# A two-layer graph kernel: each normalised tile transposed and projected one aggregation later

## The chip, the cores and the metric

The kernel runs on one core of one Trainium2 chip. The metric is the device time in microseconds. A core has five engines that run side by side and meet through semaphores: TensorE (PE, matrix products and transposes), VectorE (DVE), ScalarE (ACT), GpSimd (POOL) and SyncE (SP, which here only issues DMAs).

## The reference

The input is `x` (16 graphs, 1024 nodes, 256 features) and `adj` (16 x 1024 x 1024 integers, here 0 or 1, symmetric, with ones on the diagonal). Layer 0 is a gated aggregation, layer 1 an attention-like one; each is added to its input and normalised over the features:

```python
# layer 0: e = leaky((h * a0) @ h.T), alpha = sigmoid(e) where adj == 1 (0 elsewhere)
x = _layernorm(x + (einsum('bij,bjd->bid', alpha, h) + bias))
# layer 1
Hh = einsum('bni,io->bno', h, W); s = Hh @ a_src; d = Hh @ a_dst
e = where(adj != 0, exp(-leaky_relu(s[:, :, None] + d[:, None, :])), 0)
x = _layernorm(x + elu(einsum('bnm,bmo->bno', e, Hh) / rowsum(e)))
```

## The kernel before, in words

A graph's 1024 nodes are eight tiles of 128. The 16 graphs are passes of one loop (graph 0 and the last one are written out, 1 to 14 are the hardware loop); every engine has its own list of instructions for a pass, written out by hand in its own function `graph(b, prev, nxt)`, and the engines meet only at semaphore waits. An engine works its list strictly in this written order. `prev` and `nxt` say whether there is a graph before and behind: parts of the neighbours' work are laid between.

A pass has two halves. **Layer 0** has one step per tile t:
- PE aggregates tile t (`aggregate0`, L1154): 8 source tiles times 3 products of split numbers (`split_products`, L1097 to L1101), 24 matmuls into one of two accumulation banks (`acc_bank`). It needs the coefficients (`lo0`) and, from t = 2, that DVE has taken the residual of tile t - 2 out of its bank (`resid0`).
- DVE takes the residual (`residual0`, L822), the statistics (L827) and moments (L832); POOL computes 1/sqrt(var + eps) (`power0`, L357, L360); DVE normalises the tile into `x1` (`norm0`, L839).
- PE transposes the normalised tile (`transpose_x1`, two transposes, L1172) into `xt_bank`; ACT copies it out rounded (`high_x1T`, L551, `x1T_hi`) and DVE computes what the rounding left (`low_x1T`, L844, `x1T_lo`).
- PE projects it with W (`project`): one transpose that spreads a column of the tile before (`spread_s`, L1179), then six matmuls into `hh_bank` (L1099 to L1101). ACT takes the result out (`keep_H`, L565 to L574, four or five short steps), which frees `hh_bank` for the next projection.
- In between stand the coefficients for tile t + 3 (PE's `mirror`, L1150; DVE's `mask0_below` and `mask0_rest`, L798, L807; ACT's `high0`, L541; POOL's `low0`, L349), the transposes and splits of the next graph's x (`transpose_x`, L1107; `high_xT`, L472, L475; `low_xT`, L745, L748), chunks of its scores (`scores_chunk`; ACT's `scale_scores`, L498; DVE's `leaky_scores`, L757), and the first halves of the layer 1 coefficients (`mask1_pair`, L873).

**Layer 1** aggregates again, eight times 8 matmuls (`aggregate1`, L1213), from `H` and the coefficients, and normalises and stores.

In the kernel before, PE handles tile 0 of `x1` behind aggregation 2 and tiles 1 to 5 around aggregations 3 to 7: at step t it transposes tile t - 2 ahead of aggregation t and projects it behind it. Tiles 6 and 7 come behind the loop, with score chunks 2 to 5 of the next graph laid between. DVE's `low_x1T` and ACT's `high_x1T` and `keep_H` stand at the steps that match. `xt_bank` and `hh_bank` are single; `x1T_hi` and `x1T_lo` have two slots.

POOL's and SP's lists are not touched. SP's queue stores finished tiles and loads the next x; POOL's issues the loads of `adj`.

Of the kernel before, what the change touches and what calls it, by code (L numbers as in the profile page):

```python
# [116 lines left out]
def two_graph_layers(nc, x, adj, a0, a1, a2, a3, bias, W, a, out):  # L117
    B, N, D = x.shape
    NT = N // P
# [33 lines left out]
    with ctx:  # L153
# [309 lines left out]
        def _(act):  # L463
# [82 lines left out]
            def high_x1T(S, b, t, prev):  # L546
                act.wait_ge(S.x1T, NT * b + t + 1)

                if t >= 2 or prev:
                    act.wait_ge(S.proj, NT * b + t - 1)  # L550
                nc.scalar.activation(x1T_hi[:, t % 2, :, :],  # L551
                                     xt_bank[:, 0:D].rearrange("p (c i) -> p c i", c=KD),
                                     ACT.Copy).then_inc(S.x1T_hi, 1)
# [47 lines left out]
            def graph(b, prev, nxt):  # L601

                for t in range(NT + 1):
                    if t >= 3:
                        keep_H(F, b, t - 3, prev, False)
                    if t >= 2:
                        high_x1T(F, b, t - 2, prev)
                    if nxt and t in XT_STEP:
                        high_xT(F, b + 1, XT_STEP[t], False)
                    if t < 6:  # L610
                        watch_codes(b, t)
                    if 1 <= t and t + 3 < NT:
                        high0(F, b, t + 3, prev)
                    if t == 1 and prev:
                        norm1(F, b - 1, NT - 1)
                    if nxt and 6 <= t:
                        scale_scores(b + 1, t - 6)
                    if t in (6, 7):
                        watch_codes(b, t)

                keep_H(F, b, 6, prev, False)
                high_x1T(F, b, 7, prev)
                if nxt:
                    scale_scores(b + 1, 3)
                if nxt:
                    scale_scores(b + 1, 4)
                keep_H(F, b, 7, prev, False)
                ends_H(F, b)
                if nxt:
                    scale_scores(b + 1, 5)  # L630
                if nxt:
                    scale_scores(b + 1, 6)
                    keep_codes(F, b + 1, 0, True)
                last_G(F, b, False)
                if nxt:
                    scale_scores(b + 1, 7)
                    keep_codes(F, b + 1, 1, True)
                    high_x(F, b + 1, 0)
                    high_x(F, b + 1, 1)
                    keep_codes(F, b + 1, 2, True)  # L640

                for t in range(NT + 1):
                    if t >= 1:
                        elu_parts(F, b, t - 1)
                    if nxt and t == 0:
                        scale_scores(b + 1, 8)
                    if nxt and 1 <= t < 3:
                        tanh_row(b + 1, t - 1)
                        scale_row(b + 1, 2 + t)
                    if t + 3 >= NT and nxt:  # L650
                        high0(F, b + 1, t + 3 - NT, True)
                    if nxt:
                        if t + 3 < ACT_CODES:
                            keep_codes(F, b + 1, t + 3, True)
                        if t == 0:
                            high_x(F, b + 1, 2)
                            high_x(F, b + 1, 3)
                        if 3 <= t:
                            tanh_row(b + 1, t - 1)
                    if t >= 2:  # L660
                        norm1(F, b, t - 2)
# [55 lines left out]
        def _(dve):  # L717
# [204 lines left out]
            def graph(b, prev, nxt):  # L922

                for t in range(NT + 1):
                    if t >= 1:
                        residual0(F, b, t - 1, prev)

                    if 1 <= t < 3:
                        mask0_below(b, t + 3, prev)
                    if t >= 1:  # L930
                        stats0(F, b, t - 1)
                    if 2 <= t < 6:
                        low_x1T(F, b, t - 2)
                    if t >= 1:
                        moments0(F, b, t - 1)
                    if t >= 6:
                        low_x1T(F, b, t - 2)
                    if 3 <= t and t + 3 < NT:
                        mask0_below(b, t + 3, prev)
                    if 1 <= t and t + 3 < NT:  # L940
                        mask0_rest(b, t + 3)
                    if t == 6:
                        mask1_pair(b, 0, prev, 0, EDGE)
                    if t == 7:
                        mask1_pair(b, 2, prev, 0, EDGE)
                    if nxt and t == 5:
                        low_xT(F, b + 1, XT_STEP[t], False)
                    if t >= 1:
                        norm0(F, b, t - 1, prev)
                    if nxt and t < 5 and t in XT_STEP:  # L950
                        low_xT(F, b + 1, XT_STEP[t], False)
                    if nxt and 6 <= t:
                        leaky_scores(b + 1, t - 6)

                low_x1T(F, b, 7)
                if nxt:
                    leaky_scores(b + 1, 3)
                if nxt:
                    leaky_scores(b + 1, 4)
                mask1_pair(b, 0, prev, EDGE, NT)  # L960
                watch_sd(F, b, prev)
                if nxt:
                    leaky_scores(b + 1, 5)
                mask1_pair(b, 2, prev, EDGE, NT)
                if nxt:
                    leaky_scores(b + 1, 6)
                keep_watch(b, prev)

                for t in range(NT + 1):
                    if t >= 1:  # L970
                        row_inverse(F, b, t - 1, prev)
                    if t < 2:
                        mask1_pair(b, 2 * t + 4, prev)
                    if nxt and t == 1:
                        leaky_row(b + 1, 3)
                    if t + 3 >= NT and nxt:
                        mask0_below(b + 1, t + 3 - NT, True)
                        mask0_rest(b + 1, t + 3 - NT)
                    if nxt and ACT_CODES <= t + 3 < NT:
                        keep_codes(b + 1, t + 3)  # L980
                    if t >= 1:
                        residual1(F, b, t - 1)
                        stats1(F, b, t - 1)
                        moments1(F, b, t - 1)
                    if nxt and t in (0, 2):
                        leaky_row(b + 1, 2 + t)
# [109 lines left out]
        def _(pe):  # L1096
# [125 lines left out]
            def graph(b, prev, nxt):  # L1222

                for t in range(NT):
                    if t >= 3:

                        pe.wait_ge(F.x1T_lo, NT * b + t - 2)
                        transpose_x1(F, b, t - 2)
                    if 1 <= t and t + 3 < NT:
                        mirror(b, t + 3)  # L1230
                    aggregate0(F, b, t, prev)
                    if t == 2:
                        if prev:

                            pe.wait_ge(F.x1T_lo, NT * b)
                        transpose_x1(F, b, 0)
                    if t >= 3:
                        project(F, b, t - 2, prev)
                    if nxt and t + 1 in XT_STEP:
                        c = XT_STEP[t + 1]  # L1240
                        if c == 0:
                            pe.wait_ge(F.x_loaded, 16 * (b + 2))

                            pe.wait_ge(F.leaky, NCH * (b + 1))
                        if c >= 2:
                            pe.wait_ge(F.xT_lo, 4 * (b + 1) + c - 1)
                        transpose_x(F, b + 1, c)
                    if nxt and 5 <= t < 7:
                        if t == 5:
                            pe.wait_ge(F.xT_lo, 4 * (b + 1) + 3)  # L1250
                        else:
                            pe.wait_ge(F.xT_lo, 4 * (b + 1) + 4)
                        scores_chunk(b + 1, t - 5)
                    if t == 2:
                        project(F, b, 0, prev)

                pe.wait_ge(F.x1T_lo, NT * b + 6)
                transpose_x1(F, b, 6)
                if nxt:
                    scores_chunk(b + 1, 2)  # L1260
                    scores_chunk(b + 1, 3)
                project(F, b, 6, prev)
                pe.wait_ge(F.x1T_lo, NT * b + 7)
# [114 lines left out]
```

## Time and profile before

| | |
|---|---|
| median of 3 runs | 1476.43 us (1476.39 to 1477.39) |
| the profiled execution, its own time | 1477.27 us |
| its span, first to last instruction | 1474.8 us |
| PE busy | 1353.2 us, 92% |
| DVE busy | 1095.8 us, 74% |
| ACT busy | 934.7 us, 63% |
| POOL busy | 837.1 us, 57% |
| mean granted TensorE clock | 0.958 of full |

All 16 graphs share the span, so an average over it mixes the two halves of a pass. The share of an engine says how much it works, and not where it makes others late; for that one reads the waits, and then a single pass in order of time.

### The profile page before, as it was taken

What the parts mean: (1) busy time and instruction counts of PE and PEld (TensorE: products, weight loads), DVE (VectorE), ACT (ScalarE), POOL (GpSimd) and SP (SyncE); (2) the same over time, 40 slices, a digit from 0 to 9 for tenths busy, and PEclk for the clock granted to TensorE, in tenths of its full rate; (3) what the DMA queues carried; (4) which work ended last, traced back from release to release, by engine and by line L of the source; (5) the groups of instructions that cost most, each with busy time, mean ns of one, the idle gap of its engine ahead of it and who ended that gap; (6) DMA issues with size and microseconds to landing.
All of it is one profiled execution on the core that took longest, in us unless ns stands there. A gap on an engine that the chain in (4) does not pass through costs nothing.

```text
span 1474.8 us, 30279 instructions
## 1 busy us (share of the span) xinstructions
PE 1353.2 (92%) x9154; PEld 1231.1 (83%) x9154; DVE 1095.8 (74%) x2784; ACT 934.7 (63%) x2197; POOL 837.1 (57%) x1228
## 2 busy tenths in 40 slices
PE   4799998999989899898999989899898998989986
PEld 3688888988888798888988889798888988889875
DVE  4487876878777687776778777687777778778764
ACT  3676756657575665756757575666756756675642
POOL 3465737556484655737557383655737557384732
PEclk9799999999999999999999999999999999999988
DMA  4122130321303222131321303222121321303100
GB/s 103 30 44 64 31 67 28 50 61 32 71 15 50 65 43 64 23 53 48 50 61 32 72 15 50 65 39 64 26 50 51 50 61 26 74 19 50 36 1 31
DMA packets 55251, 68.73 MB, mean 47 GB/s; under 512 B 5488, under 2 KB 38640, under 8 KB 55152
## 3 DMA queue, kind: packets, MB, share of 16 engines
q0 software_dynamic: 18432, 33.56, 14.2%
q1 hardware_dynamic: 36720, 34.22, 7.2%
q14 instruction: 83, 0.68, 0.1%
q8 instruction: 16, 0.26, 0.1%
HBM read 84.55 MB, written 16.78 MB: 69 GB/s over the span
## 4 chain that ended last, share of the span: by engine, by line
PE 64%; DVE 13%; issue 8%; POOL 6%; DMA 5%; ACT 3%; DVEq 1%; SPq 0%; POOLq 0%; ACTq 0%
PE acc_bank L1213 23%; PE acc_bank L1099 6%; PE acc_bank L1100 6%; PE acc_bank L1101 6%; DMA code_nat<-in_adj 4%; PE lg_bank L1099 3%; PE lg_bank L1101 3%; PE lg_bank L1100 3%; DVE coef L873 3%; PE tr_bank L1134 3%; PE tr_bank L1150 3%; PE xt_bank L1172 2%; PE hh_bank L1101 2%; PE hh_bank L1099 2%; PE hh_bank L1100 2%
## 5 line engine op out<-in xcount | busy, mean ns | idle before, releaser
L1213 PE MATMUL acc_bank<-H,coef 128*128 128x258 f32 x2048 | 472.7, 384 | 9.0 <-ACT reluP L592 8.4
L1213 PEld LDWEIGHTS acc_bank<-H,coef 128*128 128x128 f32 x2048 | 383.4, 191 | 64.7 <-issue 10.9
L349 POOL TENSOR_TENSOR coef_lo<-coef,coef_hi 128x1024 fp32r<-128x1024 f32 x128 | 305.4, 2387 | 72.9 <-ACT coef_hi L541 71.7
L1099 PE MATMUL acc_bank<-h_hi,coef_hi 128*128 128x256 f32 x1024 | 309.3, 302 | 6.3 <-DVE resid L822 6.3
L1100 PE MATMUL acc_bank<-h_lo,coef_hi 128*128 128x256 f32 x1024 | 296.7, 290 | 0.0
L1101 PE MATMUL acc_bank<-h_hi,coef_lo 128*128 128x256 f32 x1024 | 295.8, 289 | 0.0
L873 DVE SCALAR_TENSOR_TENSOR coef<-G,E_col,codeT 128x256 f32<-128x256 f32 x512 | 238.0, 531 | 39.3 <-PE acc_bank L1213 36.6
L1099 PEld LDWEIGHTS acc_bank<-h_hi,coef_hi 128*128 128x128 f32 x1024 | 206.5, 202 | 9.3 <-issue 9.3
L1100 PEld LDWEIGHTS acc_bank<-h_lo,coef_hi 128*128 128x128 f32 x1024 | 206.6, 202 | 0.0
L1101 PEld LDWEIGHTS acc_bank<-h_hi,coef_lo 128*128 128x128 f32 x1024 | 205.4, 201 | 0.0
L541 ACT ACTIVATE coef_hi<-coef 128x1024 fp32r<-128x1024 f32 x128 | 136.3, 1065 | 99.0 <-DVE coef L807 98.8
L335 POOL DMA_DIRECT2D code_nat<-in_adj x128 | 73.6, 576 | 188.0 <-PE tr_bank L1134 167.3
L590 ACT ACTIVATE eluE<-acc_bank,rinv 128x256 f32<-128x256 f32 x128 | 60.8, 475 | 173.9 <-DVE rinv L897 173.9
L531 ACT ACTIVATE watch_junk<-codeT,neg_half 128x1024 bf16<-128x1024 bf16 x128 | 149.8, 1170 | 1.5
L366 POOL TENSOR_TENSOR neg_mean<-zero_col,moments 128x1 f32<-128x1 f32 x128 | 36.4, 284 | 198.7 <-DVE moments L920 198.7
L1099 PE MATMUL lg_bank<-hT_hi,gT_hi 128*128 128x384 f32 (+3 forms) x384 | 139.0, 362 | 3.9 <-DVE gT_lo L748 2.9
L498 ACT ACTIVATE score<-lg_bank 128x128 f32<-128x128 f32 (+2 forms) x192 | 95.1, 495 | 67.8 <-PE lg_bank L1101 67.7
L757 DVE TENSOR_TENSOR score<-lg_bank,score 128x128 f32<-128x128 f32 (+2 forms) x192 | 103.4, 551 | 41.5 <-ACT score L498 40.4
L1101 PE MATMUL lg_bank<-hT_hi,gT_lo 128*128 128x384 f32 (+3 forms) x384 | 132.2, 344 | 0.0
L1100 PE MATMUL lg_bank<-hT_lo,gT_hi 128*128 128x384 f32 (+3 forms) x384 | 131.6, 343 | 0.0
L357 POOL TENSOR_TENSOR var_eps<-moments,eps_col 128x1 f32<-128x1 f32 x128 | 43.0, 336 | 141.0 <-DVE moments L832 141.0
L1099 PE MATMUL hh_bank<-W_hi,x1T_hi 128*128 128x258 f32 x256 | 84.8, 331 | 27.1 <-DVE x1T_lo L844 27.1
(87 smaller groups left out, 2895.9 us busy)
## 6 DMA issues: line engine op xcount, KB each, us to landing
code_nat<-in_adj POOLq DMA_DIRECT2D x128, 256.0 KB, 3.6
x_raw<-in_x SPq DMA_DIRECT2D x16, 1024.0 KB, 5.5
out<-x SPq DMA_DIRECT2D x128, 128.0 KB, 1.7
score<-in_L_gnn_W SPq DMA_DIRECT2D x1, 256.0 KB, 2.8
score<-in_L_gnn_a SPq DMA_DIRECT2D x1, 256.0 KB, 5.8
bias_bc<-in_L_gnn_bias SPq DMA_DIRECT2D x1, 128.0 KB, 3.6
a_col<-in_L_gnn_a SPq DMA_DIRECT2D x4, 1.0 KB, 2.1
```

Of the source, the lines that this page charges most:

```text
L335: pool.dma_start(code_nat[:, t % 4, :], adj_v[b, t, :, :]).then_inc(S.adj_loaded[t % 4], 16)
L349: nc.gpsimd.tensor_tensor(coef_lo[:, t % 4, :, :], blocks(coef[:, t % 4, :]), f32(coef_hi[:, t % 4, :, :]), ALU.subtract).then_inc(S.lo0, 1)
L498: nc.scalar.activation(score_at(J, c0, c1), lg_bank[k % 2][:, 0:(c1 - c0) * P], ACT.Copy, scale=SLOPE).then_inc(F.scaled, 1)
L531: nc.scalar.activation(watch_junk[:, :], codeT[:, t, :], ACT.Square, bias=neg_half[:, :], accum_out=watch_sum[:, t:t + 1]).then_inc(F.code ...
L541: nc.scalar.activation(coef_hi[:, t % 4, :, :], blocks(coef[:, t % 4, :]), ACT.Copy).then_inc(S.hi0, 1)
L590: nc.scalar.activation(eluE[:, t % 2, :], acc_bank[t % 2][:, 0:D], ACT.Exp, scale=rinv[:, t % 2, :]).then_inc(S.elu_exp, 1)
L757: nc.vector.tensor_tensor(score_at(J, c0, c1), lg_bank[k % 2][:, 0:(c1 - c0) * P], score_at(J, c0, c1), ALU.max).then_inc(F.leaky, 1)
L873: ins = nc.vector.scalar_tensor_tensor(coef[:, at:at + 2, J * P:(J + 1) * P], blocks(G[:, t * P:(t + 2) * P]), E_col[:, J:J + 1], codeT[:, ...
L1099: nc.tensor.matmul(dst, lhs_hi, rhs_hi, start=first, stop=False)
L1100: nc.tensor.matmul(dst, lhs_hi, rhs_lo, start=False, stop=False)
L1101: return nc.tensor.matmul(dst, lhs_lo, rhs_hi, start=False, stop=last)
L1213: ins = nc.tensor.matmul(acc_bank[t % 2][:, 0:HC], coef[:, SLOT1[t], J * P:(J + 1) * P], H[:, J, :], start=J == 0, stop=J == NT - 1)
```

## The change

In layer 0 each tile of `x1` is transposed and projected one aggregation later: at step t PE transposes tile t - 3 ahead of aggregation t and projects it behind it. The special place of tile 0 behind aggregation 2 goes. Tiles 5, 6 and 7 come behind the loop, each with one score chunk between its transpose and its projection. `high_x1T`, `keep_H` (ACT), `low_x1T` and the first halves of `mask1_pair` (DVE) move by one step with it.

```diff
 # ACT, in graph()
                 for t in range(NT + 1):
+                    if t >= 4:
+                        keep_H(F, b, t - 4, prev, False)
                     if t >= 3:
-                        keep_H(F, b, t - 3, prev, False)
-                    if t >= 2:
-                        high_x1T(F, b, t - 2, prev)
+                        high_x1T(F, b, t - 3, prev)
...
+                keep_H(F, b, 5, prev, False)
+                high_x1T(F, b, 6, prev)
+                if nxt:
+                    scale_scores(b + 1, 3)
                 keep_H(F, b, 6, prev, False)
                 high_x1T(F, b, 7, prev)
-                if nxt:
-                    scale_scores(b + 1, 3)
                 if nxt:
                     scale_scores(b + 1, 4)
 # DVE, in graph()
-                    if 2 <= t < 6:
-                        low_x1T(F, b, t - 2)
+                    if 3 <= t < 6:
+                        low_x1T(F, b, t - 3)
                     if t >= 1:
                         moments0(F, b, t - 1)
                     if t >= 6:
-                        low_x1T(F, b, t - 2)
+                        low_x1T(F, b, t - 3)
...
-                    if t == 6:
+                    if t == 7:
                         mask1_pair(b, 0, prev, 0, EDGE)
-                    if t == 7:
+                    if t == 8:
                         mask1_pair(b, 2, prev, 0, EDGE)
...
+                low_x1T(F, b, 6)
+                if nxt:
+                    leaky_scores(b + 1, 3)
                 low_x1T(F, b, 7)
-                if nxt:
-                    leaky_scores(b + 1, 3)
 # PE, in graph()
                     if t >= 3:
-
-                        pe.wait_ge(F.x1T_lo, NT * b + t - 2)
-                        transpose_x1(F, b, t - 2)
+                        if t > 3 or prev:
+                            pe.wait_ge(F.x1T_lo, NT * b + t - 3)
+                        transpose_x1(F, b, t - 3)
                     if 1 <= t and t + 3 < NT:
                         mirror(b, t + 3)
                     aggregate0(F, b, t, prev)
-                    if t == 2:
-                        if prev:
-
-                            pe.wait_ge(F.x1T_lo, NT * b)
-                        transpose_x1(F, b, 0)
                     if t >= 3:
-                        project(F, b, t - 2, prev)
+                        project(F, b, t - 3, prev)
...
-                    if t == 2:
-                        project(F, b, 0, prev)
-
+
+                pe.wait_ge(F.x1T_lo, NT * b + 5)
+                transpose_x1(F, b, 5)
+                if nxt:
+                    scores_chunk(b + 1, 2)
+                project(F, b, 5, prev)
                 pe.wait_ge(F.x1T_lo, NT * b + 6)
                 transpose_x1(F, b, 6)
                 if nxt:
-                    scores_chunk(b + 1, 2)
                     scores_chunk(b + 1, 3)
                 project(F, b, 6, prev)
```

## Rows read from the trace of the kernel before

**Rows 1.** The page, part 1: busy time, share of the span, instructions

```profile
PE 1353.2 (92%) x9154; PEld 1231.1 (83%) x9154; DVE 1095.8 (74%) x2784; ACT 934.7 (63%) x2197; POOL 837.1 (57%) x1228
```

**Rows 2.** PE's waits in total: us, times, longest us

```profile
PE xt_bank L1172 <- DVE x L839: 27.3, 22, 1.7
PE hh_bank L1099 <- DVE x1T_lo L844: 27.1, 16, 1.9
```

**Rows 3.** PE in order of time, graph 7: start, us, what [idle before <- releaser]

```profile
687.62 0.41 PE L1172 MATMUL xt_bank<-ident,x 128*128 128x128 f32 x2
...
690.38 0.39 PE L1099 MATMUL hh_bank<-W_hi,x1T_hi 128*128 128x258 f32 x1 [1.91 <-DVE x1T_lo L844]
...
693.02 0.66 PE L1172 MATMUL xt_bank<-ident,x 128*128 128x128 f32 x2 [1.38 <-DVE x L839]
...
693.55 0.56 PE L1099 MATMUL acc_bank<-h_hi,coef_hi 128*128 128x256 f32 x1
...
698.33 0.27 PE L1179 MATMUL hh_bank<-ident,sd 128*128 128x128 f32 x1
...
699.76 0.36 PE L1099 MATMUL acc_bank<-h_hi,coef_hi 128*128 128x256 f32 x1
...
702.59 0.27 PE L1179 MATMUL hh_bank<-ident,sd 128*128 128x128 f32 x1
...
708.30 0.41 PE L1172 MATMUL xt_bank<-ident,x 128*128 128x128 f32 x2
...
776.20 0.41 PE L1172 MATMUL xt_bank<-ident,x 128*128 128x128 f32 x2
```

**Rows 4.** Stretches: length, busy PE, PEld, DVE, ACT, POOL, granted clock, DMA, GB/s

```profile
158.40:162.30 3.90, 2.41 (x20) 2.35 (x21) 3.42 (x9) 3.90 (x12) 3.24 (x3) 1.00 0.00 0
...
687.50:691.00 3.50, 1.59 (x12) 1.26 (x11) 1.88 (x6) 2.85 (x7) 3.09 (x4) 0.99 0.11 37
691.00:697.60 6.60, 5.22 (x26) 4.96 (x25) 6.08 (x15) 5.46 (x14) 5.93 (x7) 0.50 0.00 1
...
1445.30:1448.70 3.40, 3.07 (x7) 2.52 (x8) 1.88 (x7) 1.71 (x5) 1.34 (x6) 0.50 0.11 39
```

**Rows 5.** DVE in order of time, graph 7, same columns as rows 3

```profile
687.06 0.41 DVE L839 TENSOR_SCALAR x<-resid,moments,rstd 128x256 f32<-128x256 f32 x1 [0.61 <-POOL rstd L360]
688.91 0.42 DVE L822 SCALAR_TENSOR_TENSOR resid<-acc_bank,xb 128x256 f32<-128x256 f32 x1 [1.44 <-ACT x L598]
...
692.07 0.81 DVE L839 TENSOR_SCALAR x<-resid,moments,rstd 128x256 f32<-128x256 f32 x1 [0.44 <-POOL rstd L360]
...
694.18 0.41 DVE L822 SCALAR_TENSOR_TENSOR resid<-acc_bank,xb 128x256 f32<-128x256 f32 x1
...
694.97 0.41 DVE L844 TENSOR_TENSOR x1T_lo<-xt_bank,x1T_hi 128x256 fp32r<-128x256 f32 x1
...
700.52 0.43 DVE L844 TENSOR_TENSOR x1T_lo<-xt_bank,x1T_hi 128x256 fp32r<-128x256 f32 x1 [0.68 <-ACT x1T_hi L551]
...
704.78 0.41 DVE L822 SCALAR_TENSOR_TENSOR resid<-acc_bank,xb 128x256 f32<-128x256 f32 x1
...
714.04 2.15 DVE L873 SCALAR_TENSOR_TENSOR coef<-G,E_col,codeT 128x256 f32<-128x256 f32 x4
```

**Rows 6.** The last link of graph 7's tail, projection 6 to projection 7

```profile
719.37 0.28 PE L1179 MATMUL hh_bank<-ident,sd 128*128 128x128 f32 x1
...
720.41 0.17 ACT L565 ACTIVATE scale_col<-hh_bank 128x1 f32<-128x1 f32 x1 [1.74 <-PE hh_bank L1101]
...
721.10 0.42 ACT L551 ACTIVATE x1T_hi<-xt_bank 128x256 fp32r<-128x256 f32 x1
...
721.55 0.42 DVE L844 TENSOR_TENSOR x1T_lo<-xt_bank,x1T_hi 128x256 fp32r<-128x256 f32 x1 [1.33 <-ACT x1T_hi L551]
...
722.03 0.32 PE L1179 MATMUL hh_bank<-ident,sd 128*128 128x128 f32 x1
```

**Rows 7.** PE, graph 1, the transpose of tile 1

```profile
159.89 0.41 PE L1172 MATMUL xt_bank<-ident,x 128*128 128x128 f32 x2 [1.51 <-DVE x L839]
```

More of the change, by code:

```diff
@@ L953, in graph @@
                         leaky_scores(b + 1, t - 6)
-                low_x1T(F, b, 7)
+                low_x1T(F, b, 6)
                 if nxt:
                     leaky_scores(b + 1, 3)
+                low_x1T(F, b, 7)
                 if nxt:
```

## The prediction

> Names: T(k), P(k) and N(k) are the transpose, the projection and the normalising of tile k of x1; A(k) is the aggregation of tile k in layer 0; hi(k) and lo(k) are ACT's and DVE's halves of the transposed tile (L551, L844); R(k) is DVE's residual (L822). A graph is one pass of the loop; times are those of graph 7 unless said otherwise.
>
> **What bounds the kernel now.** I read the page first: PE is busy for 92% of the span, DVE as the next for 74% [rows 1]. So the question is what PE waits for. The table of PE's waits puts two lines above all others, and both touch the change: T waits 27.3 us for DVE's N, P waits 27.1 us for DVE's lo [rows 2]. By time they are the same pair in each graph: after A(2), P(0) idles 1.91 us for lo(0), and T(1) then 1.38 us for N(1); only then, at 693.55, does A(3) start [rows 3]. The stretch table adds a cost that no wait shows: in the 6.6 us from 691.0 the granted clock is 0.50 of full, the lower level, with PE busy for 5.22 us of them; ahead of it PE had been busy for only 1.59 of 3.5 us [rows 4]. So some 2.6 us of matmul time are lost there beside the 3.3 us of waiting.
>
> Is PE the limit there? The DVE timeline says no. R(1) starts at 688.91, R(2) at 694.18, R(4) at 704.78 [rows 5]: 5.3 us per tile, while A(2) had ended by 687.6. An aggregation takes 2.83 us at full clock (699.76 to 702.59) and a whole PE step 4.26 us (P(1) at 698.33, P(2) at 702.59) [rows 3]. In these steps DVE sets the pace and PE waits in whatever place the order puts the wait. That decides the case: the change reorders PE more than it relieves DVE.
>
> **The change, part by part.** The three engines issue the same instructions; nothing is added or removed, POOL's and SP's lists are untouched, and no moved step issues a DMA. What moves is where PE meets DVE.
>
> Head on PE. T(0) and P(0) leave the place behind A(2). A(3) then needs only R(1), which frees its bank: 688.91 + 0.42 = 689.33 [rows 5], with some 0.15 us from DVE to PE as between N(1) (692.07 + 0.81) and T(1) (693.02) [rows 3, 5]. It starts at 689.5, 4.1 us earlier than now, after some 1.1 us of idle, and ends at 692.3. This is the gain.
>
> Next is P(0), now behind A(3), and it needs lo(0). DVE now does lo(0) in the step that follows, behind R(2) and its statistics. R(2) comes earlier only by what the removed lo(0) held up, at most its own 0.41 us; since N(1) waits for rstd from POOL in between (0.44 us [rows 5]), not all of it may come through. Between 0 and 0.41 I take 0.29. Thus R(2) at 693.9, lo(0) at 694.97 - 0.29 = 694.7, done at 695.1 [rows 5]. P(0) starts at 695.15 instead of 690.38 [rows 3], after 2.85 us of idle: one wait, longer than either of the two it replaces. What ran ahead of lo(0) there before, DVE's split of the next graph's x, now stands in front of it.
>
> From there DVE paces on: it regains the 0.68 us for which lo(2) waited now [rows 5]. A(4) 696.5 to 699.4; P(1) waits for lo(1) until 699.9 (0.55 us); A(5) 701.35 to 704.2; P(2) waits for lo(2) until 705.0 (0.78 us); A(6) starts at 706.6, now 708.45 (right behind T(4) at 708.30 [rows 3]). That is 1.85 us earlier, but PE owes one tile (T and P, 0.15 + 0.85 us) more than now: the real lead is 0.8 us.
>
> Tail. Now two tiles are left behind A(7), after the change P(4) and three pairs. A bare link P(k) to P(k+1), where PE ends up waiting for it, is 722.03 - 719.37 = 2.66 us [rows 6]: keep_H's five ACT steps (720.41 to 721.10), hi (0.42), lo (0.42) [rows 6]. P, T and the score chunk between take 2.15 us with chunk 2, 2.4 us with 3 or 4. After: A(7) ends at 714.05, P(4) to 714.9, and P(5) starts a link later, 716.75 (0.55 us idle). For P(6) DVE is later than the link: first half of mask1_pair(2) (2.15 us [rows 5]), N(7), leaky of chunk 2 and then lo(6), 716.65 + 2.15 + 0.4 + 0.4 + 0.4, done at 720.0; P(6) starts at 720.05 (0.9 us idle). P(7) one link later, 722.8 (0.4 us idle). Now P(7) starts at 722.03 with 0.2 us of idle. **So each graph ends 0.8 us later**, even with no clock loss at all: the tail gives back the lead twice. The work behind P(7) is bound by PE as now, and DVE's and ACT's lists there are the same.
>
> Clock. The 0.8 us is for a full clock after the change against the drop before it. No row shows the new pattern, so bounds. If the clock never drops: 0. If it drops for 6.6 us as now: up to 3.3 us of matmul time, of which P(1)'s and P(2)'s waits (1.3 us) swallow part: 2.0. A drop of half that length occurs, 3.4 us at 0.50 in the last graph [rows 4]: 1.7 - 1.3 = 0.4. Against "never": ahead of today's drop PE idled 1.9 us [rows 4], and the new wait is 2.85 us. Against "always, in full": in graph 1 a wait of 1.51 us led to no drop ([rows 7]; its stretch is at 1.00 [rows 4]); and behind P(0) the new order has no second wait of 1.38 us that keeps PE idle in the slow stretch. I take 0.6 us, near the short drop.
>
> **The Trainium skill** speaks against this change too ("TensorE: Matmul & The Clock Gate", section "HAM oscillation — how this bites in real kernels"): a wait for data that comes once in each pass of a loop throttles the array anew every pass, and the work behind it starts slow. The trace agrees where it can, a drop beside the pair of waits in graph 7, and graph 1 shows the exception. Taken at its word, every pass pays in full; that is rival 1.
>
> First and last graph. Graph 0 has the same order: 0.8. The last has no next graph, so no chunk covers the tail: three bare links instead of two, +2.66 us, against the tile deferred (1.0) and a shorter head, since its waits of the same kind as graph 7's mostly go. I take 0, between -1 and +2.
>
> Sum: 15 x 0.8 = 12; 14 x 0.6 = 8.4; together 20.4 us. The profiled execution took 1477.3 us (span 1474.8 and 2.5 around it): 1497.7. The median of the runs is 0.8 us lower, so I predict 1497 us.
>
> **Rivals.**
> 1. The clock stays as bad as now or worse. Place: behind P(0) in every graph. Price 2.0 us instead of 0.6: 15 x 0.8 + 14 x 2.0 = 40, 1516 us. For it: the single wait is longer, the drop comes in graph 7 after less. Against: the missing second wait. It decides if PE's slow stretch in the new trace is still 6.6 us.
> 2. The tail is covered. The waits at P(5) and P(6), 1.45 us, rest on ACT and DVE orders to within tenths; if both are hidden, a graph is 0.65 us shorter before the clock's 0.6: 1476 us, no change. Against: two tiles already leave P(7) waiting.
> 3. The other side, faster: DVE steps shrink. Place: DVE between R(2) and R(5). N takes 0.81 us there against 0.41 at 687.06 [rows 5], and each step idles 0.44 us for rstd. If lo's new place lines these up, up to 0.8 us per step go, 2.4 us over three: 20.4 - 15 x 2.4 = -16, 1461 us. It decides from 1.4 us per graph, 0.45 us a step. Against: N, mask0 and POOL's low0 keep their order, and PE, not DVE, is the later one from A(6) on, so part would be lost.
> 4. That PE was the limit in these steps after all, so that A(3)'s 4.1 us lead stays: 1477 - 15 x 2 = 1447 us. R(2) at 694.18, 6.6 us after A(2), speaks against it; I give it nothing of its own beyond rival 3.
>
> **How the numbers follow.** Forecast 0.56, rival 1 0.26, rival 2 0.08, rivals 3 and 4 together 0.10. What this kernel's measurement can tell from no change is about 0.2%, 3 us: faster 0.10, same 0.07, slower 0.83 (a little of rival 2 falls on the slower side). The forecast's own range is 1487 (no clock loss) to 1508; the range asked for reaches up to rival 1 and down short of no change: 1481 to 1517.
>
> **What would show it.** Right: A(3) follows A(2) within some 2 us; P(0) shows one wait of about 2.8 us for L844, the largest of PE's waits, and T's wait for N (27.3 us) is nearly gone; new waits of P on L844 of 0.3 to 0.9 us at tiles 1, 2, 5, 6, 7; T(0) of graph 7 to the first transpose of graph 8, now the time from one graph to the next, grows from 88.6 us (687.62 to 776.20 [rows 3]) to about 90. Wrong head: P(0)'s wait under 2 us. Wrong tail: P(5) and P(6) without a wait. Wrong clock: no stretch at 0.50, or 6.6 us in every graph. The forecast falls if that time is under 88.6 us.

## The result, and the profile after

The changed kernel takes 1502.03 us (median of 4 runs, 1500.32 to 1503.92), the kernel before 1476.91 us beside it (4 runs, 1476.39 to 1479.38): ratio 1.0167 with a 95% interval of 1.0149 to 1.0185, 25.1 us slower. The profiled execution took 1503.92 us, its span is 1501.8 us against 1474.8. The forecast was 1497 us in a range of 1481 to 1517.

The page of the changed kernel, part 1 (busy us, share of the span, instructions):

```profile
PE 1346.0 (90%) x9154; PEld 1215.0 (81%) x9154; DVE 1106.7 (74%) x2784; ACT 936.1 (62%) x2197; POOL 837.6 (56%) x1228
```

Same instructions, 27.0 us more span, and yet PE is busy for 7.2 us less [rows 1]. So PE waits more, and runs at the low clock less (mean granted clock 0.975 of full against 0.958). The table of its waits (us in total, times, longest) says for what:

```profile
PE hh_bank L1102 <- DVE x1T_lo L846: 39.3, 16, 2.6
PE hh_bank L1182 <- DVE x1T_lo L846: 38.5, 45, 1.5
PE acc_bank L1102 <- DVE resid L824: 20.0, 26, 1.1
```

The line that led the table before, T waiting for N with 27.3 us, is gone. P(0)'s wait for lo(0) grew from 27.1 [rows 2] to 39.3 us. New are P's waits for lo at the other tiles (L1182 stands first in every projection but P(0)): 38.5 us in 45 waits, against 2.8 us before. A's wait for the residual went from 6.3 to 20.0 us. In sum 97.8 us against 63.5 us: 34.3 us more waiting, less 7.2 us of busy time, is 27.1 us, and the span grew by 27.0.

PE in order of time, graph 7 (start, us, what, idle before and its releaser):

```profile
699.73 0.38 PE L1175 MATMUL xt_bank<-ident,x 128*128 128x128 f32 x2
...
701.19 0.36 PE L1102 MATMUL acc_bank<-h_hi,coef_hi 128*128 128x256 f32 x1 [0.97 <-DVE resid L824]
...
706.78 0.39 PE L1102 MATMUL hh_bank<-W_hi,x1T_hi 128*128 128x258 f32 x1 [2.52 <-DVE x1T_lo L846]
...
728.56 0.32 PE L1182 MATMUL hh_bank<-ident,sd 128*128 128x128 f32 x1 [0.36 <-DVE x1T_lo L846]
...
732.67 0.32 PE L1182 MATMUL hh_bank<-ident,sd 128*128 128x128 f32 x1 [1.46 <-DVE x1T_lo L846]
```

R(1) of this graph starts at 700.62, 11.71 us later than before (688.91 [rows 5]). Less that shift, A(3) starts at 689.48 (forecast 689.5) and P(0) at 695.07 (forecast 695.15). P(5) waits 0.36 us (forecast 0.55), P(6) 1.46 us (forecast 0.9). The same stretch on DVE and POOL shows why P(6) is late:

```profile
728.08 0.42 DVE L846 TENSOR_TENSOR x1T_lo<-xt_bank,x1T_hi 128x256 fp32r<-128x256 f32 x1 [0.34 <-ACT x1T_hi L551]
728.42 3.07 DVE L875 SCALAR_TENSOR_TENSOR coef<-G,E_col,codeT 128x256 f32<-128x256 f32 x4
728.63 0.86 POOL L344 TENSOR_TENSOR xb<-x_raw,bias_bc 128x256 f32<-128x256 f32 x1
729.44 0.59 POOL L335 DMA_DIRECT2D code_nat<-in_adj  x1
730.05 0.75 POOL L344 TENSOR_TENSOR xb<-x_raw,bias_bc 128x256 f32<-128x256 f32 x1
731.41 0.40 DVE L841 TENSOR_SCALAR x<-resid,moments,rstd 128x256 f32<-128x256 f32 x1
731.74 0.54 DVE L759 TENSOR_TENSOR score<-lg_bank,score 128x384 f32<-128x384 f32 x1
732.21 0.41 DVE L846 TENSOR_TENSOR x1T_lo<-xt_bank,x1T_hi 128x256 fp32r<-128x256 f32 x1
```

ACT's high half of tile 6 was done at 730.8. DVE, with its list in fixed order, was still at the four mask steps: 3.07 us, where the same four took 2.15 us [rows 5]. They now lie beside POOL's additions of the next graph's bias (L344) and its DMA issue. Taken one by one, the first and the last of the four take 0.47 us; the second and the third are the long ones:

```profile
728.81 0.96 DVE L875 SCALAR_TENSOR_TENSOR coef<-G,E_col,codeT 128x256 f32<-128x256 f32 x1
729.69 1.40 DVE L875 SCALAR_TENSOR_TENSOR coef<-G,E_col,codeT 128x256 f32<-128x256 f32 x1
```

The second ends 0.28 us after POOL's first addition (at 729.49), the third 0.29 us after the second addition (at 730.80).

Clock. Three stretches of the changed kernel, behind P(0) of graphs 7, 8 and 9 (length, busy PE, PEld, DVE, ACT, POOL, granted clock, DMA, GB/s):

```profile
707.90:711.20 3.30, 3.30 (x18) 3.30 (x18) 3.27 (x8) 2.96 (x9) 2.77 (x3) 0.54 0.00 0
798.50:801.80 3.30, 2.91 (x27) 2.72 (x26) 3.27 (x9) 3.30 (x10) 2.76 (x2) 1.00 0.00 0
889.00:892.30 3.30, 3.30 (x19) 3.30 (x19) 3.27 (x9) 3.30 (x10) 2.77 (x3) 0.57 0.00 0
```

At the low level (1.2 GHz) 18 or 19 matmuls run in 3.3 us, at the high one (2.4 GHz) 27. The slow stretch behind P(0) is now 3.4 us long instead of 6.8 and comes in 10 of the 14 graphs between the first and the last (1, 3, 5, 7 and 9 to 14), where the kernel before had it in 13 (2 to 14).

Where a graph gains and loses shows best in distances from R(1), as means over graphs 2 to 13. They are worked out from the DVE rows of residual and low half in each kernel's timeline; the last column is from one graph's R(1) to the next:

```
us after the start of R(1)     R(2)   R(4)   R(6)   R(7)   lo(5)  lo(6)  lo(7)  period
before                         5.27  15.99  23.37  27.97  24.90  29.21  32.74   88.84
changed                        4.91  14.87  20.99  25.91  27.42  31.55  34.24   90.42
```

The head leads by 2.4 us at R(6), the tail turns it into a loss of 1.5 us at lo(7). The time from lo(7) to the next R(1) is nearly the same (56.09 and 56.18).

### The profile page after: what moved, and what is told of

The parts are those of the page before. It is cut to its first block, busy times and chain, and to the rows that moved or that the text cites. A ratio compares the mean times of both kernels' runs of the same rounds, so it can differ in the third digit from the quotient of the medians.

```text
span 1501.8 us, 30279 instructions
## 1 busy us (share of the span) xinstructions
PE 1346.0 (90%) x9154; PEld 1215.0 (81%) x9154; DVE 1106.7 (74%) x2784; ACT 936.1 (62%) x2197; POOL 837.6 (56%) x1228
## 4 chain that ended last, share of the span: by engine, by line
PE 54%; DVE 18%; POOL 10%; issue 9%; DMA 4%; ACT 3%; DVEq 1%; POOLq 0%; SPq 0%; ACTq 0%
PE acc_bank L1216 22%; DVE coef L875 6%; POOL coef_lo L349 4%; DMA code_nat<-in_adj 4%; PE acc_bank L1102 4%; PE acc_bank L1103 3%; PE acc_bank L1104 3%; PE lg_bank L1102 3%; PE lg_bank L1104 3%; PE lg_bank L1103 3%; PE tr_bank L1137 3%; PE tr_bank L1153 2%; POOL rstd L360 2%; PE hh_bank L1102 2%; PE hh_bank L1104 2%
## 5 line engine op out<-in xcount | busy, mean ns | idle before, releaser
L1102 PE MATMUL acc_bank<-h_hi,coef_hi 128*128 128x256 f32 x1024 | 301.1, 294 | 20.1 <-DVE resid L824 20.0
L1103 PE MATMUL acc_bank<-h_lo,coef_hi 128*128 128x256 f32 x1024 | 289.1, 282 | 0.0
L1104 PE MATMUL acc_bank<-h_hi,coef_lo 128*128 128x256 f32 x1024 | 288.6, 282 | 0.0
L875 DVE SCALAR_TENSOR_TENSOR coef<-G,E_col,codeT 128x256 f32<-128x256 f32 x512 | 246.9, 547 | 39.3 <-PE acc_bank L1216 36.6
L1102 PEld LDWEIGHTS acc_bank<-h_hi,coef_hi 128*128 128x128 f32 x1024 | 198.2, 194 | 26.0 <-issue 26.0
L1103 PEld LDWEIGHTS acc_bank<-h_lo,coef_hi 128*128 128x128 f32 x1024 | 198.1, 193 | 0.0
L1104 PEld LDWEIGHTS acc_bank<-h_hi,coef_lo 128*128 128x128 f32 x1024 | 197.3, 193 | 0.0
L1102 PE MATMUL hh_bank<-W_hi,x1T_hi 128*128 128x258 f32 x256 | 85.7, 335 | 39.3 <-DVE x1T_lo L846 39.3
L809 DVE SCALAR_TENSOR_TENSOR coef<-score,codeT 128x512 f32<-128x512 f32 (+1 forms) x192 | 111.3, 607 | 3.4 <-issue 3.4
```

What stands on the lines that cost most here:

```text
L809: ins = nc.vector.scalar_tensor_tensor(blocks(coef[:, t % 4, j0 * P:j1 * P]), score[:, 0:j1 - j0, at:at + P], 1.0, blocks(codeT[:, t, j0 * ...
L875: ins = nc.vector.scalar_tensor_tensor(coef[:, at:at + 2, J * P:(J + 1) * P], blocks(G[:, t * P:(t + 2) * P]), E_col[:, J:J + 1], codeT[:, ...
L1102: nc.tensor.matmul(dst, lhs_hi, rhs_hi, start=first, stop=False)
L1103: nc.tensor.matmul(dst, lhs_hi, rhs_lo, start=False, stop=False)
L1104: return nc.tensor.matmul(dst, lhs_lo, rhs_hi, start=False, stop=last)
```

## The experiments

All ran against the kernel before on the same chip (1476.7 to 1478.3 us). For each, the ratio is to that kernel.

**Mask steps late.** Changed kernel, DVE's first half of mask1_pair(2) moved behind the last low halves:

```diff
-                    if t == 8:
-                        mask1_pair(b, 2, prev, 0, EDGE)
...
-                mask1_pair(b, 2, prev, EDGE, NT)
+                mask1_pair(b, 2, prev, 0, NT)
```

> The changed kernel with one thing moved on DVE: the first half of mask1_pair(2) (four instructions of step 8) is taken out of step 8 and done together with its second half, behind lo(7). Theory T (tail): in the changed kernel P(6) waits 1.46 us per graph because lo(6) stands behind that half, which takes 3.07 us there. Without it lo(6) follows hi(6) at once, P(6) starts one bare link (2.66 us) after P(5), 1.4 us earlier, and so does P(7): 15 x 1.4 = 21 us less than 1502, about 1481 us. Rival H (head): the loss lies in the single wait of 2.5 us at P(0); then the tail is slack and the time stays within 3 us of 1502. Rival L (later): the moved work makes the layer 1 aggregation wait, and a part of the 1.4 us comes back there: 1485 to 1502 us, with a new wait of L1216 for L875.

Measured: 1482.42 us (1478.83 to 1484.75), ratio 1.0033 (1.0020 to 1.0047): 19.6 us less than the changed kernel. PE's waits of this run:

```profile
PE hh_bank L1100 <- DVE x1T_lo L846: 40.5, 16, 2.7
...
PE acc_bank L1100 <- DVE resid L824: 19.9, 26, 1.1
PE hh_bank L1180 <- DVE x1T_lo L846: 17.8, 32, 1.4
```

The second and third line swapped places: P's waits behind P(0) fell from 38.5 to 17.8 us, 20.7 us, which is the gain (19.6 us); the head's two lines moved by 1.2 us or less. This is Theory T. lo(7) comes at 32.91. In graph 7 P(6) and P(7) follow at the bare link of 2.71 us:

```profile
718.50 0.32 PE L1180 MATMUL hh_bank<-ident,sd 128*128 128x128 f32 x1 [0.36 <-DVE x1T_lo L846]
...
721.21 0.32 PE L1180 MATMUL hh_bank<-ident,sd 128*128 128x128 f32 x1
...
723.92 0.32 PE L1180 MATMUL hh_bank<-ident,sd 128*128 128x128 f32 x1
```

Four DVE instructions in front of lo(6) make most of the 25 us.

**The same edit on the kernel before**, as a control (there the steps stand at t == 7).

> Control: the kernel before, with the second half-pair of mask steps (4 of DVE's scalar-tensor-tensor, 2.15 us, ahead of N(6)) moved behind the last low half, the same edit that took 19.6 us off the changed kernel. Theory A (in the kernel before the last link starts from R(7), and N(6) has room): no gain, 1474 to 1479 us. Rival B (these steps cost the kernel before as well, so that the edit says nothing of the change): 1460 us or less. Rival C (late mask steps disturb layer 1): above 1480 us.

Measured: 1473.22 us (1471.43 to 1477.52), 0.9973 (0.9964 to 0.9982). Just below Theory A's range, so not quite nothing: 4.7 us, 0.3 us per graph, against 19.6 us in the changed kernel. They are there already at R(2), which comes at 4.90 instead of 5.27. In the kernel before the moments behind R(1) had an idle of 0.20 us that the view puts down to no wait, and rstd and N(1) came later with it:

```profile
690.53 0.18 DVE L832 BATCH_NORM_AGGREGATE moments<-stats 128x2 f32<-128x6 f32 x1 [0.20 <-issue]
```

The control has these moments right behind lo(0) (687.85, graph 7, no idle; R(1) at 686.52) and N(1) 2.78 us after R(1) instead of 3.16. In both kernels the first DVE step behind such an idle starts about 0.1 us after the end of POOL's `low0` (690.46 here, 688.06 in the control, where the moments came ahead of that end); no run tests whether that is the cause. From R(2) to lo(7) the edit gave the kernel before nothing (27.54 and 27.47 us). So what the same edit takes off the changed kernel between R(2) and lo(7) (29.33 and 27.89 us, 1.4 us per graph) belongs to the place that the change gave the steps.

**POOL's additions late.** Changed kernel, the bias additions of the ninth step and the last one issued three DMAs later:

```diff
-                    if nxt and t >= 2:
+                    if nxt and 2 <= t < NT:
...
                 if nxt:
-                    next_bias(b, NT - 1)
                     for t in range(4, 7):
                         load_adj(F, b + 1, t, False)
+                    next_bias(b, NT - 2)
+                    next_bias(b, NT - 1)
```

> The changed kernel with POOL's last two additions of the bias (L344, for tiles 6 and 7, each 0.75 to 0.86 us) moved behind its next three loads of adj, so that they no longer run beside DVE's first half of mask1_pair(2). Theory C (contention): the four DVE instructions take 3.07 us there and 1.67 us elsewhere because POOL's two additions run beside them; without these they take about 2 us, lo(6) and P(6) come 1.0 us earlier: 1487 us. Rival D (it is the DMA issue of POOL that slows them, or the place itself): 3.07 us stays, 1502 us.

Measured: 1500.93 us (1500.38 to 1501.57), 1.0162 (1.0145 to 1.0179). The contention is shown: without POOL's additions beside them the four mask steps take 1.66 us in graph 7, not 3.07, P(6) has no wait, and lo(7) comes at 32.80, as with the steps moved away. One DMA issue of POOL still lies beside them (726.49 to 727.08, the steps 726.26 to 727.92), so Rival D falls too. But the time stayed, and Theory C's 1487 us with it. PE's waits of this run say where it went:

```profile
PE acc_bank L1217 <- ACT reluP L593: 27.2, 16, 2.8
...
PE hh_bank L1183 <- DVE x1T_lo L847: 19.2, 34, 1.4
```

The tail's waits fell by 19.3 us as before, and layer 1's wait for ACT rose from 8.4 to 27.2, 18.8 us. The additions now run where layer 1 begins, ahead of POOL's split of the next x (L340), which comes 1.4 us later after lo(7) for it. DVE's eight masks there now begin beside two of the split's steps instead of only its last one (graph 7, POOL and DVE, this run and then the changed kernel):

```profile
742.47 1.43 POOL L344 TENSOR_TENSOR xb<-x_raw,bias_bc 128x256 f32<-128x256 f32 x2
743.85 4.97 POOL L340 TENSOR_TENSOR h_lo<-x_raw,h_hi 128x512 fp32r<-128x512 f32 x4
746.46 5.41 DVE L876 SCALAR_TENSOR_TENSOR coef<-G,E_col,codeT 128x256 f32<-128x256 f32 x8 [2.24 <-PE acc_bank L1217]
...
746.02 4.98 POOL L340 TENSOR_TENSOR h_lo<-x_raw,h_hi 128x512 fp32r<-128x512 f32 x4
750.01 4.05 DVE L875 SCALAR_TENSOR_TENSOR coef<-G,E_col,codeT 128x256 f32<-128x256 f32 x8 [2.24 <-PE acc_bank L1216]
```

The eight masks take 1.36 us more, all of it in the first of them (2.64 us, against 1.28), and from lo(7) to the next R(1) it takes 57.39 us instead of 56.18. That layer 1's longer wait comes from these slow masks rather than from POOL's other late steps is argued from the order and the sizes, not shown by a run.

**lo(0) early.** Changed kernel, hi(0) and lo(0) back in the step after T(0), so that P(0) waits for neither:

```diff
-                    if 3 <= t < 6:
-                        low_x1T(F, b, t - 3)
+                    if t == 2:
+                        low_x1T(F, b, 0)
+                    if 4 <= t < 6:
+                        low_x1T(F, b, t - 3)
```

(ACT's high_x1T alike.)

> The changed kernel, but with tile 0's hi (ACT) and lo (DVE) back at step 2, where they were before the change; PE's list stays as changed. P(0)'s wait of 2.5 us should go in both theories. Theory T (DVE paces the head, PE only waits somewhere): the residuals R(2) to R(5) come at the same times, the wait turns up at A(4) and P(1), and the time is 1497 to 1502 us (only the clock may gain up to 0.3 us per graph). Rival H (PE's wait adds to the time): 15 x 2.4 = 36 us less, 1466 us.

Measured: 1516.3 us (1515.62 to 1519.46), 1.0269 (1.0252 to 1.0286). Slower than the changed kernel by 14 us, which neither theory had. The longest wait of the kernel was taken away, and others took more than its place:

```profile
PE hh_bank L1186 <- DVE x1T_lo L848: 70.5, 53, 2.8
PE lg_bank L1114 <- DVE gT_lo L752: 20.7, 17, 3.4
```

PE did P(0) at once and arrived early at the transposes of the next graph's x, where it waits for gT_lo (20.7 us in all, 4.0 in the changed kernel), and P(1) waits 2.2 us for lo(1). R(2) comes at 5.28, with the idle of 0.20 us ahead of the moments, both as in the kernel before, and lo(7) at 35.11, 0.9 us later than in the changed kernel; where the other 0.5 us, between R(2) and lo(7), come from is open. PE's wait at P(0) was the visible end of another engine's pace, not a cost of its own; Rival H, by which it was, would have had 1466 us.

**Fillers.** To see what the low clock costs, TensorE does transposes of the identity in the time in which it would wait at P(0). In the kernel before 14 of them, in the changed one 20 (2.34 us by the row below):

```diff
+                if S is F and t == 0:
+                    if prev:
+                        pe.wait_ge(S.H, NT * b)
+                        pe.wait_ge(S.G, NT * b)
+                    for _ in range(14):
+                        nc.tensor.transpose(hh_bank[:, 0:P], ident[:, :], ident[:, :])
                 pe.wait_ge(S.x1T_lo, NT * b + t + 1)
```

> The kernel before, with 14 extra transposes of the identity (a full bank's quarter, about 0.11 us each by the kernel's own four-transpose groups of 0.6 us, so 1.5 us in all) put on TensorE ahead of P(0)'s wait for DVE's low half in layer 0 of every graph; they write a place in hh_bank that P(0) writes afterwards. Question: what the low granted clock after the 1.9 us of waiting at P(0) costs the kernel before. Theory A, TensorE's speed between P(0) and A(4) sets the pace: the 6.8 us stretch at 0.50 goes, matmuls there run at 0.12 instead of 0.21 us spacing, and each of 13 graphs gains about half of the stretch that isn't waiting, 1.5 to 2.0 us: 1450 us (1446 to 1458). Theory B, DVE's steps (about 5.0 us each from R(1) to R(4)) set the pace there and the slow clock only fills waits: 1470 to 1478 us, with new waits of TensorE for resid as long as the time that the faster matmuls save.

Measured on the kernel before: 1467.93 us (1462.67 to 1469.36), 0.9943 (0.9930 to 0.9956), 9.7 us faster. The stretch of graph 7 in which the clock was 0.50 [rows 4] is now at 1.00 throughout; five other graphs (4, 5, 8, 9 and 13) keep one of 3.4 us:

```profile
682.00:700.00 18.00, 15.15 (x126) 14.21 (x125) 15.44 (x37) 15.87 (x41) 15.99 (x16) 1.00 0.02 8
```

Between the two theories: 0.75 us per graph over 13, where Theory A had 1.5 to 2.0. R(2) and R(3) did not move (5.27, 10.05), T waits 33.0 us for N instead of 27.3; only from R(4) on is it 0.7 us earlier (15.29 against 15.99). Part of the matmul time that the full clock saved went into waits for DVE.

> The changed kernel with 20 such transposes (2.2 us) ahead of P(0)'s wait of 2.5 us. Question: the share of the clock in the changed kernel's 25 us. Theory A: the 3.4 us stretches at 0.50, which stand in about 9 graphs of the changed kernel, go, and each costs 0.4 to 0.8 us: 1495 to 1498 us. Theory B: DVE's steps set the pace of the head, so that the clock costs it nothing: 1501 to 1503 us, with A(5) and A(6) at the same distances from R(1). Rival C, that the clock is the larger part of the loss: below 1490 us.

Measured on the changed kernel: 1502.2 us (1500.27 to 1504.25), 1.0176 (1.0159 to 1.0192). Nothing gained that the intervals could tell, Theory B. The fillers ran (graph 7), no stretch at 0.50 is left in graphs 1 to 14, and PE waits more for lo:

```profile
703.09 2.34 PE L1191 MATMUL hh_bank<-ident 128*128 128x128 f32 x20
```

```profile
PE hh_bank L1182 <- DVE x1T_lo L846: 48.8, 63, 1.5
PE acc_bank L1102 <- DVE resid L824: 19.5, 26, 1.1
```

That line was 38.5. The new waits are those of P(1) and P(2) in the graphs that had a slow stretch: in graph 7, where neither waited, they now wait 0.40 and 0.74 us, and P(5) and P(6) wait 0.36 and 1.46 us as before. R(4) comes at 14.89 (14.87 without fillers), R(6) at 20.96 (20.99). In the changed kernel the low clock costs nothing that these runs can tell, since the next thing PE needs comes from DVE and comes no earlier.

**Both, late mask steps and fillers.**

> The changed kernel with both edits: the four mask steps of DVE after the ninth step moved behind the last low halves (as in the run that moved them alone, 1482.4 us), and the 20 extra transposes ahead of P(0). If clock and tail are independent, their effects add: by Theory A of the run with the transposes alone 1482 minus 4 to 7 = 1475 to 1478 us; by Theory B 1482 us. In the run with the late mask steps nearly every graph had a 3.4 us stretch at 0.50, so by Theory A up to 15 x 0.7 = 10 us less: 1472 us at the lowest. P(6) has no wait for x1T_lo in either.

Measured: 1484.38 us (1483.17 to 1484.99), 1.0051 (1.0037 to 1.0065): no less than the late mask steps alone (1482.4). Theory A falls; lo(7) at 32.91 in both.

**Catch up in the tail.** Changed kernel, A(7) in two halves with P(4), T(5) and lo(5) between, so that the order of the kernel before holds again from P(5) on; the mask steps stand behind lo(6).

```diff
-                    aggregate0(F, b, t, prev)
+                    aggregate0(F, b, t, prev, 0, NT // 2 if t == 7 else NT)
...
                 transpose_x1(F, b, 5)
-                if nxt:
-                    scores_chunk(b + 1, 2)
+                aggregate0(F, b, 7, prev, NT // 2, NT)
                 project(F, b, 5, prev)
```

> The changed kernel with its tail cut back to two tiles: the last aggregation of layer 0 is split in two halves of 12 matmuls each, P(4) stands between them, and T(5), second half, P(5) follow, so that behind the loop only tiles 6 and 7 are left with chunks 2 and 3 between T(6) and P(6), as in the kernel before; ACT and DVE are ordered to match, the first half of mask1_pair(2) stands behind lo(6). Theory T: the head of the changed kernel leads by about 0.6 us per graph and only the third tile in the tail loses (2.1 us); with the tail of before it is faster than before: 1477 - 15 x 0.6 = 1468 us, 1463 to 1474. Rival H (the head is no faster): 1477 or above. Rival L: DVE is late for N(7) or lo(7), T(7) or P(7) wait over 0.5 us more than before: 1477 to 1485.

Measured: 1479.33 us (1477.19 to 1481.91), 1.0014 (1.0005 to 1.0024), 23 us less than the changed kernel but not below the kernel before; Theory T's 1468 us is missed, and Rival L comes nearest. R(7) comes at 26.76, 1.2 us earlier than before, lo(7) at 32.83, 0.1 us later: lo(6) stood behind N(7) and a score step on DVE. With the fillers added:

> The changed kernel with A(7) split in halves between P(4) and P(5) and with P(5) to P(7) in the places of the kernel before (1479.3 us without the extra transposes, with a 3.4 us stretch at 0.50 in nearly every graph), and the 20 extra transposes ahead of P(0). Theory A (the head's lead was eaten by the low clock): 1479 less 15 x 0.7 to 15 x 1.0 = 1464 to 1469 us, which would beat the kernel before. Theory B (DVE's steps pace the head, so there was no lead to eat): 1477 to 1480 us, with the matmuls faster and the waits for resid longer by the same.

1479.79 us (1475.61 to 1480.88), 1.0014 (1.0004 to 1.0024): Theory B again.

**Tail forward.** The same head and split; on DVE lo(6) ahead of N(7), the mask steps late, and score chunks 3 and 4 each one place later on TensorE (diff against the catch-up version, TensorE only):

```diff
                 transpose_x1(F, b, 6)
                 if nxt:
                     scores_chunk(b + 1, 2)
-                    scores_chunk(b + 1, 3)
...
                 transpose_x1(F, b, 7)
                 if nxt:
-                    scores_chunk(b + 1, 4)
+                    scores_chunk(b + 1, 3)
                 project(F, b, 7, prev)
                 if nxt:
+                    scores_chunk(b + 1, 4)
                     scores_chunk(b + 1, 5)
```

> A version meant to be faster: the changed kernel's head, A(7) split in halves with P(4) and T(5) between, and in the tail the score chunks 3 and 4 of the next graph each one place later on TensorE, so that P(6) has one chunk ahead of it instead of two; on DVE lo(6) goes ahead of N(7) and the four mask steps of the ninth step go behind the last low halves. In the split version measured (1479.3 us) lo(6) came 30.15 us and lo(7) 32.83 us after R(1), though the last residual stood at 26.76. Theory A (the chain from the last residual sets the end, 4.77 us to lo(7) in the kernel before): lo(7) at 31.0 to 31.5, so 1.3 to 1.8 us per graph less: 1453 to 1460 us. Rival B (the scores that P(7) no longer covers come later and are on the path after P(7), before layer 1): the gain is given back there, 1474 to 1480 us. Rival C (DVE's mask steps, late, delay layer 1): 1465 to 1474 us.

Measured: 1497.29 us (1489.62 to 1501.89), 1.0130 (1.0108 to 1.0152), a miss. The part that was aimed at worked, lo(7) at 31.56, 1.2 us ahead of the kernel before. But from lo(7) to the next R(1) it now takes 58.4 us instead of 56.1. PE's waits show two of the places:

```profile
PE acc_bank L1218 <- ACT reluP L592: 12.2, 16, 2.8
...
PE lg_bank L1102 <- DVE score L760: 7.7, 17, 0.5
```

Chunk 4, 1.4 us of matmuls, lies behind P(7) now instead of covering a link; chunk 7 waits 0.5 us for DVE's step on chunk 5, which stands behind four mask steps; and layer 1's wait for ACT is 0.2 us longer (12.2 us in all against 8.4). These three make up 2.1 of the 2.3 us. It is Rival B, and worse than that by 17 us. With the fillers, no difference beyond the spread of the two:

> The same with the 20 extra transposes ahead of P(0), which took every stretch at 0.50 out of graphs 2 to 14 of the other versions with this head and moved their times by under 2 us. If DVE paces this head: the time of the version without them, within 2 us. If with a shorter tail TensorE sets the pace in the head as well: 3 to 8 us less.

1494.69 us (1490.35 to 1497.99), 1.0121 (1.0106 to 1.0137).

**A version without the change**, the kernel before with its fillers and the late mask steps:

> A version without the change: the kernel before with both edits that helped it alone, the 14 extra transposes ahead of P(0) (1467.9 us, 0.9943 of the time before) and the four mask steps behind the last low half (1473.2 us, 0.9973). Theory A, the two gains are in different places (A(3) and A(4) at the full clock; R(2) and the last link 0.3 us earlier) and add: 1462 to 1465 us, ratio 0.991 to 0.993. Theory B, both gains shorten the same chain and only the larger counts: 1466 to 1469 us.

Measured: 1464.82 us (1459.95 to 1465.55), 0.9904 (0.9890 to 0.9918). Theory A: the gains add, and of all versions run this is the fastest.

## Why the forecast came out as it did

- **DVE paces the head: right in what it says of PE.** A(3)'s start and P(0)'s are within 0.1 us of the forecast, R(2) came 0.36 us earlier (forecast 0.29), T's waits are gone and P(0)'s wait, 2.52 us here and 2.6 at most, heads the table. The run with lo(0) early shows the reason: the wait can be moved, and the pace stays. The reason given for R(2) was luck in part: the forecast took it from the lo(0) that goes, but the control still has lo(0) there and its R(2) comes at the same 4.90. And no run separates DVE from POOL, which is busy for 4.44, 4.10 and 5.06 us of the three steps from R(1) to R(4) (4.91, 4.77 and 5.20 us; DVE 4.42, 4.69 and 4.72 us, graph 7).
- **A(6) 1.85 us earlier: nearly right.** A(6) starts at 718.53, less the shift 706.82 (forecast 706.6), 1.63 us earlier. P(1) and P(2), which were to wait 0.55 and 0.78 us, wait 0.39 and 0.73 us in graph 8, at the full clock; in graph 7, where the slow matmuls fill that time, they do not wait. A(3)'s idle, for the residual, is 0.97 us (forecast 1.1).
- **The tail: mechanism right, size wrong.** P(5) and P(6) wait for lo, as forecast, and P(6) waits behind mask1_pair(2)'s half. That half was taken from the kernel before, 2.15 us; in its new place it takes 3.07 us, and so it does, to 0.01 us, in all 15 graphs that have a next one. That is 0.92 us more per graph. In graph 7 P(6) starts at 720.96 less the shift (forecast 720.05) and P(7) at 723.65 (forecast 722.8, before 722.03); over graphs 2 to 13 lo(7) is late by 1.50 us instead of 0.8. The forecast priced a moved step by its duration at the old place and did not ask what runs on POOL at the new one. The run with POOL's additions moved gives 1.66 us for the same four steps.
- **The clock: wrong term, 0.6 us per graph taken, 0 measured.** The slow stretch got shorter and rarer, inside the bounds, but the step that failed is the assumption that a slow stretch adds its matmul time to the end. With fillers in the changed kernel the stretches go and the time stays (1502.2 us). In the kernel before, where the stretch is 6.8 us long and reaches R(4), fillers that took it away or halved it gained 9.7 us.
- **First and last graph: wrong, small.** Graph 0 was taken at 0.8 us and the last at nothing, between -1 and +2. From R(1) to the next R(1) graph 0 takes 2.55 us more, graph 1 1.9, graph 14 1.3; the last graph takes 2.4 us more from its R(1) to the end of the span. No run takes these apart.
- The errors offset each other, and the nearness of 1497 to 1502 is luck to that extent: 0.8 + 0.6 us per graph was forecast, about 0.8 + 0.8 + 0 happened (the period grew by 1.58 us). In the profiled executions the first 15 graphs make 24.8 us of the span's 27.0, the last one 2.4; the medians are 25.1 us apart.
- **Rival 1**, by the rule of the Trainium skill ("TensorE: Matmul & The Clock Gate", section "HAM oscillation — how this bites in real kernels") that every pass pays, did not come: in graph 8 PE idles at P(0) as in graphs 7 and 9, and the stretch behind it is at 1.00. **Rival 2**, the covered tail, did not come by itself, since both waits are there; the late mask steps take the one at P(6) away (1482.4 us, 0.33% above the kernel before). **Rival 3**, shorter DVE steps: R(4) to R(6) come 1.1 to 2.4 us earlier, but a lead there was in the sum already, and N still takes 0.6 us on average. **Rival 4**, PE as the limit in these steps, did not come: A(3) starts 4.1 us earlier and R(2) only 0.36.

## What to carry to other kernels

When a step moves, look up what the other engines run at its new place before taking its old duration: four DVE steps grew from 2.15 to 3.07 us beside GpSimd's additions, and 15 times 0.92 us would be 14 of the 25 us. The same goes for the edit that is to mend it: with the additions moved away the four steps took 1.66 us, and the time came back in layer 1. A wait of one engine can be the place where another engine's pace becomes visible; here, removing P(0)'s wait without shortening that other engine's list made the kernel 14 us slower. A lead in the middle of a loop is worth what the last chain of the pass leaves of it: 2.4 us at R(6) were a loss of 1.5 us at lo(7).

## What was not expected of the hardware

- Four DVE scalar-tensor-tensor steps of 128x256 take 1.66 us with GpSimd's adder idle, 2.15 us in the kernel before, beside one GpSimd addition of 128x256, and 3.07 us beside two, which themselves take 0.86 and 0.75 us. The growth from 1.66 to 3.07, 1.41 us, is near the 1.61 us of these two. It lies in single steps: a mask step takes 0.47 to 0.49 us or ends 0.28 to 0.29 us after the end of a GpSimd tensor step beside it. That holds for all 45 mask steps over 0.55 us in the kernel before, all 60 in the changed kernel and all 30 with the additions late, where one step took 2.64 us beside two steps of GpSimd's split of x. The Trainium skill ("SBUF — State Buffer", section "SBUF: two separate sides") says of the port pair that DVE and GpSimd share that it is an exclusive lock: the later of two such steps, here a DVE step with two inputs in SBUF against a GpSimd step that reads it, waits for the whole of the other. The ends agree with that. The order does not everywhere: the mask step of 1.40 us began at 729.69 and the addition for whose end it seems to have waited only at 730.05.
- With a wait of 2.5 us at the same place in every graph the granted clock fell to 0.50 for 3.4 us in ten of 14 graphs of the changed kernel (every second one up to graph 9, then every one) and stayed at 1.00 behind P(0) in the others; with 1.9 and 1.4 us of waiting close together, in the kernel before, it fell for 6.8 us in every graph from 2 to 14.
- 14 transposes of the identity per graph, work that computes nothing, made the kernel before 9.7 us faster; 20 of them made the changed kernel no faster.
